# Moving the product with A between the two tiles of every pair, and reordering the prologue of an AdaLN + LoRA feed-forward kernel

## What is computed

```
cond  = grouped_conv1d(x, weight, taps=9, pad=4, groups=4) + (cond_128 @ c_weight.T)[:, :, None] + fside_S_0[None, :, None]
base  = cond @ kernel + bias                        # kernel is 1024 x 1024
A_eff = einsum('bn,nri->bri', gate, lora_A)         # 8 batches of 8 samples, rank 32
B_eff = einsum('bn,nor->bor', gate, lora_B)
delta = (cond @ A_eff.T) @ B_eff.T + (cond @ lora_A_shared.T) @ lora_B_shared.T
out   = x + base + delta
```

## Time and profile before

| | us |
|---|---|
| median of 3 runs (lowest, highest) | 515.07 (512.89, 516.81) |
| the profiled execution | 516.11 |
| its span, first to last instruction | 514.3 |

### The profile page before, as it was taken

The page is one execution under the profiler, slowest core; times in us unless marked ns, Lnnn a source line. Parts: engine busy times, 40 slices in busy tenths (PEclk is TensorE's granted clock), DMA queues, the critical chain, the costliest instruction groups (busy, mean ns, idle before and its releaser), DMA issues.

```text
span 514.3 us, 6831 instructions
## 1 busy us (share of the span) xinstructions
PE 494.3 (96%) x2400; PEld 406.6 (79%) x2400; DVE 342.0 (67%) x389; ACT 165.8 (32%) x207; POOL 269.7 (52%) x154
## 2 busy tenths in 40 slices
PE   4988899989999999999999999999999999999995
PEld 3755598868888888888888888888888888888884
DVE  3988767887938495767948495758848495754411
ACT  2545422341423233331423234331523234331000
POOL 1567861993746338471756347571757247571100
PEclk9999899998999999999999999999999999999999
DMA  8995196852763419331753328331753413232212
GB/s 211 312 234 213 40 264 155 177 203 85 157 164 89 112 43 197 112 105 64 171 155 82 112 54 193 111 100 61 174 152 82 112 50 88 65 97 71 80 40 72
DMA packets 19575, 65.05 MB, mean 126 GB/s; under 512 B 3274, under 2 KB 3914, under 8 KB 18922
## 3 DMA queue, kind: packets, MB, share of 16 engines
q1 hardware_dynamic: 17690, 63.46, 47.1%
q10 hardware_dynamic: 1872, 1.41, 1.1%
HBM read 45.59 MB, written 18.87 MB: 125 GB/s over the span
## 4 chain that ended last, share of the span: by engine, by line
PE 89%; DVE 6%; POOL 1%; DMA 1%; issue 1%; ACT 1%; ACTq 0%; DVEq 0%
PE main L926 65%; PE rank L939 6%; PE main L931 3%; PE conv L856 3%; PE conv L880 2%; PE conv L881 2%; PE conv L882 2%; PE spare L882 1%; PE spare L881 1%; PE spare L880 1%; DMA cw_nat<-in_L_cond_c_weight 1%; DVE y_lo L666 1%; POOL y_lo L379 1%; DVE w_raw L678 1%; POOL x_lo L367 1%
## 5 line engine op out<-in xcount | busy, mean ns | idle before, releaser
L926 PE MATMUL main<-w_hi,y_hi 128*128 128x512 f32 x512 | 160.8, 393 | 1.8 <-POOL w_lo L384 1.1
L926 PE MATMUL main<-w_lo,y_hi 128*128 128x512 f32 x512 | 159.8, 391 | 0.4 <-POOL w_lo L384 0.4
L926 PE MATMUL main<-w_hi,y_lo 128*128 128x512 f32 x512 | 159.5, 390 | 0.0
L379 POOL TENSOR_TENSOR y_lo<-y_stage,y_hi 128x512 fp32r<-128x512 f32 x56 | 89.0, 1611 | 85.5 <-ACT y_hi L481 85.5
L926 PEld LDWEIGHTS main<-w_lo,y_hi 128*128 128x128 f32 x512 | 96.6, 189 | 21.7 <-POOL w_lo L384 0.8
L926 PEld LDWEIGHTS main<-w_hi,y_hi 128*128 128x128 f32 x512 | 95.9, 189 | 22.5 <-issue 2.5
L926 PEld LDWEIGHTS main<-w_hi,y_lo 128*128 128x128 f32 x512 | 96.4, 188 | 20.5
L367 POOL TENSOR_TENSOR x_lo<-x_tr,x_hi 128x1024 fp32r<-128x1024 f32 x28 | 82.2, 2935 | 21.4 <-ACT x_hi L494 21.4
L365 POOL TENSOR_TENSOR xd_lo<-xd,xd_hi 128x512 fp32r<-128x512 f32 x28 | 45.7, 1634 | 55.0 <-ACT xd_hi L492 55.0
L494 ACT ACTIVATE x_hi<-x_tr 128x1024 fp32r<-128x1024 f32 x28 | 57.4, 2049 | 30.2 <-DVE x_tr L642 30.2
L481 ACT ACTIVATE y_hi<-y_stage 128x512 fp32r<-128x512 f32 x56 | 35.5, 633 | 95.6 <-DVE y_stage L660 95.6
(11 more groups left out here) (104 smaller groups left out, 496.0 us busy)
## 6 DMA issues: line engine op xcount, KB each, us to landing
res<-in_x SPq DMA_DIRECT2D x32, 512.0 KB
out<-res SPq DMA_DIRECT2D x31, 512.0 KB
x_in<-in_x SPq DMA_DIRECT2D x28, 512.0 KB, 11.8
w_raw<-in_L_ffn_kernel SPq DMA_DIRECT2D x16, 256.0 KB, 18.6
b_cur<-b_scratch SPq DMA_DIRECT2D x21, 128.0 KB, 2.4
la<-in_L_ffn_lora_A SPq DMA_DIRECT2D x4, 512.0 KB, 10.4
lb<-in_L_ffn_lora_B SPq DMA_DIRECT2D x1, 2048.0 KB, 18.0
b_scratch<-be_hi SPq DMA_DIRECT2D x4, 256.0 KB, 8.6
```

The source lines that it names most:

```text
L379: nc.gpsimd.tensor_tensor(y_parity(y_lo, h, t, e), y_staged(e), y_parity(y_hi, h, t, e).bitcast(F32), ALU.subtract).then_inc(ylo_done, 1)
L926: mm(main[t][:, n * 512:(n + 1) * 512], lhs, rhs[:, k, n * 512:(n + 1) * 512], start=k == 0 and first, stop=False)
```

## The change

1. In every unit PE's `with_a(h)` moves from behind k = 3 of tile 0 to behind k = 7, between the tiles; `fast` of tile 0 stays where it was. `lowrank(0)` moves behind k = 2 of tile 1, `fast` of tile 1 follows it. ACT, DVE and POOL lists follow: the y parts of tile 0 come first, then the rank steps, then x; in unit 1 ACT does both `x_high(2, 0, t)` ahead of `ax_high(1)`, DVE both `x_diff` ahead of `ax_steps(1)`.
2. `chunk(k)` of the prologue does the two products with the rounded W (`w_hi`) for both tiles first and waits for `w_lo` only then; `chunk(1)` and `chunk(2)` are ahead of `convolve(0, 0, 2)` and `(0, 0, 3)`.
3. DVE does `w_add(0..3)` and the `a_turn`s ahead of `x_turn(0, 4..7)`.
4. The low parts of y of unit 0 (`y_first_low`, four subtractions of 128x512) move from DVE to POOL (`y_low_first`); POOL's order of `be_low(0)` and w_low(4..6) shifts. The low part of t01 stays on DVE but moves to behind `finish(0, 1)`; ACT keeps a copy of the raw taps for it (`t01_kept`, one more 128x512 pass).

The diff, cut to its core:

```
@@ POOL
+            def y_low_first(i):
+                t, mh = FIRST[i]
+                pool.wait_ge(yhi_done, i + 1)
+                nc.gpsimd.tensor_tensor(y_part(y_lo, 0, t, mh), y_stage[:, i % 2, :],
+                                        y_part(y_hi, 0, t, mh).bitcast(F32), ALU.subtract).then_inc(y0_lo, 1)
...
             pool.wait_ge(bias_split, 2)
+            y_low_first(0)
+            y_low_first(1)
             w_low(0)
             w_low(1)
             x_first_low(1)
             w_low(2)
+            y_low_first(2)
             w_low(3)
+            y_low_first(3)
+            w_low(4)
             x_low_second(0)
-            w_low(4)
+            w_low(5)
             x_low_second(1)
             a_low(0)
-            w_low(5)
-            w_low(6)
-            for b4 in range(RQ):
...
+            be_low(0)
+            w_low(6)
+            for b4 in range(1, RQ):
+                be_low(b4)
             w_low(7)
@@ ACT
             nc.scalar.activation(t01_hi[:, :, :, :], t01_raw[:, :, :, :], ACT.Copy).then_inc(t01_split, 1)
+            nc.scalar.activation(t01_kept[:, :, :, :], t01_raw[:, :, :, :], ACT.Copy).then_inc(t01_split, 1)
...
             def unit(b, h, y=True, low=True, rank_first=True):
                 u = b * 2 + h
-                if rank_first:
-                    ax_high(u)
-                if low and h == 1:
-                    a_high(b + 1)
-                if y:
-                    for t in range(2):
+                for t in range(2):
+                    if y:
                         y_high(u + 1, 1 - h, 2 * t)
                         y_high(u + 1, 1 - h, 2 * t + 1)
-                        if low:
-                            x_high(u + 2, h, t)
+                    if t == 0 and rank_first:
+                        ax_high(u)
+                        if low and h == 1:
+                            a_high(b + 1)
+                    if low:
+                        x_high(u + 2, h, t)
...
-            ax_high(1)
             x_high(2, 0, 0)
             x_high(2, 0, 1)
+            ax_high(1)
+            a_high(1)
@@ DVE
             y_tile(0, 0, 1, FIRST, first=True)
+            a_turn(0)
             nc.vector.tensor_tensor(t01_raw ...
-            dve.wait_ge(x_first[1], 64)
-            x_turn(0, 4)
-            a_turn(0)
-            x_turn(0, 5)
             a_turn(1)
-            y_first_low(0)
-            y_first_low(1)
-            x_turn(0, 6)
-            x_turn(0, 7)
             w_add(0)
             w_add(1)
             a_turn(2)
-            a_turn(3)
             w_add(2)
             w_add(3)
-            x_first_low(1)
+            a_turn(3)
+            dve.wait_ge(x_first[1], 64)
+            for c in range(XH, XC):
+                x_turn(0, c)
             w_add(4)
             w_add(5)
+            x_first_low(1)
...
             def unit(b, h, y=True, turn=True, begun=False):
+                if begun:
+                    finish(b, 2 * h)
+                if y:
+                    y_pair(nb, nh, 0)
                 if not begun:
                     ax_steps(u)
-                if y:
-                    y_pair(nb, nh, 0)
                 if turn and h == 0:
                     x_turns(b + 1, 0, XC)
-                finish(b, 2 * h)
+                if not begun:
+                    finish(b, 2 * h)
...
             finish(0, 1)
+            dve.wait_ge(t01_split, 2)
+            nc.vector.tensor_tensor(t01_lo[:, :, :, :], t01_kept[:, :, :, :], t01_hi[:, :, :, :].bitcast(F32), ...
             x_turns(1, 0, XC)
             x_diff(2, 1, 0, 0)
+            x_diff(2, 1, 0, 1)
             ax_steps(1)
-            x_diff(2, 1, 0, 1)
@@ PE
             mix_a(2)
-            mix_a(3)
             merge(2)
             merge(3)
+            mix_a(3)
...
+            def chunk(k):
+                pe.wait_ge(y0_lo, 2 if k < 4 else 4)
+                pe.wait_ge(whi_done, k + 1)
+                for t in range(2):
+                    if k == 0 and t == 1:
+                        pe.wait_ge(a_done, RQ)
+                    dense(0, t, k, products=(0, 2))
+                pe.wait_ge(wlo_done, k + 1)
+                for t in range(2):
+                    dense(0, t, k, products=(1,))
...
+            chunk(0)
             merge(4)
             merge(5)
+            chunk(1)
             convolve(0, 0, 2, FIRST, first=True)
-            chunk(1)
             merge(6)
             merge(7)
+            chunk(2)
             convolve(0, 0, 3, FIRST, first=True)
-            chunk(2)
...
                 for k in range(4):
                     dense(h, 0, k)
+                if y and not late:
+                    fast(nb, nh, 0)
+                for k in range(4, KC):
+                    dense(h, 0, k)
                 pe.wait_ge(ylo_done, u * CT)
                 pe.wait_ge(acur_done, b + 1)
                 pe.wait_ge(ax_summed, u)
                 with_a(h)
-                if y and not late:
-                    fast(nb, nh, 0)
-                for k in range(4, KC):
-                    dense(h, 0, k)
-                pe.wait_ge(axlo_done, u + 1)
-                ...
-                lowrank(0)
                 pe.wait_ge(main_free, u * 2)
...
                 for k in range(3):
                     dense(h, 1, k)
+                first_rank()
                 if y:
                     fast(nb, nh, 0 if late else 1)
-                for k in range(3, 5):
+                for k in range(3, 6):
                     dense(h, 1, k)
                 if y and late:
                     fast(nb, nh, 1)
-                for k in range(5, KC):
+                for k in range(6, KC):
                     dense(h, 1, k)
                 lowrank(1)
```

More of the change, by code:

```diff
@@ L97, in adaln_ffn @@
         a_cur = sb("a_cur", [P, KC, 2, R], F32R)
-        t01_hi, t01_lo = sb("t01_hi", [P, G, J, CG], F32R), sb("t01_lo", [P, G, J, CG], F32R)
+        t01_hi = sb("t01_hi", [P, G, J, CG], F32R)
+        t01_kept, = early(("t01_kept", [P, G, J, CG], F32))
+        t01_lo = sb("t01_lo", [P, G, J, CG], F32R)
         lb, = early(("lb", [P, 2, 2048], F32))
@@ L400, in _, with be_low @@
             w_low(2)
+            y_low_first(2)
             w_low(3)
+            y_low_first(3)
+            w_low(4)
             x_low_second(0)
-            w_low(4)
+            w_low(5)
             x_low_second(1)
             a_low(0)
-            w_low(5)
-            w_low(6)
-            for b4 in range(RQ):
+            def be_low(b4):
                 pool.wait_ge(be_hid, b4 + 1)
@@ L417, in unit @@
                 u = b * 2 + h
-                if low and h == 1:
-                    a_low(b + 1)
-                if y:
-                    for t in range(2):
+                for t in range(2):
+                    if y:
                         y_low(u + 1, 1 - h, 2 * t)
                         y_low(u + 1, 1 - h, 2 * t + 1)
-                        if low:
-                            x_low(u + 2, h, t)
+                    if low and h == 1 and t == 0:
+                        a_low(b + 1)
+                    if low:
+                        x_low(u + 2, h, t)
             x_low(2, 0, 0)
@@ L661, in y_pair @@
                                         y_add[:, e, :].rearrange("p (a m n) -> p a n m", a=2, n=SB)).then_inc(y_turned, 1)
[L663 to L667, removed]
             def x_first_low(half):
@@ L793, in _ @@
             finish(0, 1)
+            dve.wait_ge(t01_split, 2)
+            nc.vector.tensor_tensor(t01_lo[:, :, :, :], t01_kept[:, :, :, :], t01_hi[:, :, :, :].bitcast(F32),
+                                    ALU.subtract).then_inc(t01_split, 1)
             x_turns(1, 0, XC)
             x_diff(2, 1, 0, 0)
+            x_diff(2, 1, 0, 1)
             ax_steps(1)
-            x_diff(2, 1, 0, 1)
             unit(0, 1, begun=True)
@@ L874, in fast @@
                     pe.wait_ge(conv_free, 2 * CT)
-                    pe.wait_ge(t01_split, 2)
+                    pe.wait_ge(t01_split, 3)
                 for part in (SUM, EVEN, ODD):
@@ L954, in _ @@
             mix_a(2)
-            mix_a(3)
             merge(2)
             merge(3)
[L959 to L964, removed]
-            pe.wait_ge(t01_sum, 1)
[L968 to L975, removed]
+            mix_a(3)
[7 more added lines that the diff above has]
+                pe.wait_ge(wlo_done, k + 1)
+                for t in range(2):
+                    dense(0, t, k, products=(1,))
+            pe.wait_ge(t01_sum, 1)
+            chunk(0)
             merge(4)
             merge(5)
+            chunk(1)
             convolve(0, 0, 2, FIRST, first=True)
-            chunk(1)
             merge(6)
             merge(7)
+            chunk(2)
             convolve(0, 0, 3, FIRST, first=True)
-            chunk(2)
             merge(8)
@@ L1007, in _ @@
             convolve(0, 1, 3)
-            chunk(7, (0,))
+            pe.wait_ge(wlo_done, KC)
+            dense(0, 0, KC - 1)
```

(19 more changed lines are left out.)

8 lines of the change are left out of this document (1 added, 7 removed).

## The result

Five runs of each kernel on one chip: 512.79 us median (512.05 to 513.78) against 516.81 (512.89 to 517.16), a ratio of 0.9938, 95% interval 0.9911 to 0.9966 (the two medians alone give 0.9922). The kernel is faster by 0.6%, 3.2 us by that ratio, where 7.4 had been forecast.

A forecast was written before the change was run, and what follows sets the result against it. PE works in 96% of the span, so only its waits, slow clock and two ends can be won back. Unit 2 -3.7, unit 1's earlier start -5.4, a clock fall +1.7: -7.4, from 515.07 to 507.7 us, range 503.5 to 512.

The forecast's parts named there:

- Unit 2's wait and clock, -3.7: In unit 2, `with_a`'s wait for POOL's `y_lo` and the slow clock behind it go: -3.7 us.
- The short run ahead of `lowrank(0)` costs nothing in the steady state: Steady units: 4.10 us of matmuls cover a rank chain of 2.16 us, slack 1.9, so price nothing, 14 times.
- Unit 1 begins at 72.4: End of prologue: POOL's list frees main[0] at 72.4, so unit 1 begins then and not at 77.85: -5.4 us.
- PE's own list ends at 70.2: End of prologue: PE's work from B_eff's turns at 53.6 takes 16.5 us, so PE then waits 2.2 us.
- The clock after that wait, +1.7: Start of unit 1: PE's wait of 2.2 us lowers the clock, charged +1.7 us (bounds 0 and 1.7).
- R3: Unit 1: rank chain misses its 0.4 us slack before `lowrank(0)`; 2.4 wait plus 1.7 clock, 511.8 us; chance 0.10.
- R2: Prologue: `lb`, issued later, lands at 50.0 instead of 45.25; PE arrives at 74.9, two clock falls, 510.2 us; chance 0.10.
- DVE is relieved by the move of y's low parts: Prologue: DVE loses four subtractions to POOL, one of which took 3.38 us beside POOL's `x_lo`; POOL gains 5.2 us.

The follow-up runs named there:

- experiment 7: Only the units' new lists on the prologue of before, with the old order in unit 1, against the kernel before: 511.62 us, ratio 0.9922.
- experiment 8: Changed kernel with `lowrank(0)` behind one chunk of tile 1 instead of three, in every unit but the last: 531.52 us, ratio 1.0304 to the kernel before.
- experiment 5: Changed kernel with the old order in unit 1 and POOL waiting for DVE's rank low part ahead of `y_low_second(0)`: 508.16 us, ratio 0.9861 to the kernel before.
- experiment 3: The new prologue alone, with the units' order of before, against the kernel before: 513.52 us, ratio 0.9945.
- experiment 2: All new unit lists, with the new order in unit 1, on the prologue of before, against the kernel before: 517.21 us, ratio 1.0021.
- experiment 4: Changed kernel with POOL waiting for DVE's low part of unit 0's rank product ahead of `y_low_second(0)`: 512.24 us, ratio 0.9936 to the kernel before.
- Experiment 1: Changed kernel with unit 1's old order, rank steps ahead of the second x step on ACT and DVE: 510.22 us, ratio 0.9889 to the kernel before.
- experiment 6: As experiment 5, but the four low parts of y of unit 0 back on DVE: 507.77 us, ratio 0.9845 to the kernel before.
- 9: As experiment 5, with DVE's `finish(0, 0)` ahead of `y_tile(0, 1, 3)`: 506.95 us, ratio 0.9827 to the kernel before.
- experiment 10: As experiment 5, with `mix_b` behind chunk 4 instead of chunk 3: 507.37 us, ratio 0.9838 to the kernel before.

## Why the prediction was wrong

507.7 us with a range of 503.5 to 512.0 was forecast and 512.79 measured: the direction was right, the size more than twice too large (7.4 against 3.2 us by the ratio).

- **Unit 2's wait and clock, -3.7:** right. Shown by the trace after and alone by experiment 7 (4.0).
- **The short run ahead of `lowrank(0)` costs nothing in the steady state:** right. Units are 28.75 apart, and the slack that was put at 1.9 us measured 1.8 (experiment 8).
- **"Unit 1 begins at 72.4":** wrong by 2.3 us in the profiled execution, and this is the first step that failed. POOL's list was right: `y_low_second(0)`, the first of the two `y_lo` from 66.73, ended near 68.0, as worked out. But DVE's list had a second claim that was left out, put at nothing without a reason: its rank subtraction L766 stands between `y_tile(0, 1, 1)` and `y_tile(0, 1, 2)`, and beside a POOL that never pauses it took 4.06 us, so the eviction that was to be done by 68 began at 69.64. The sum had priced such a meeting in unit 1 and in the steady units, and not here, where POOL was said in the same paragraph to have no gap. Where the meeting ended at the first boundary, by chance (experiment 8: 1.31 us, unit 1 at 72.28) or by the wait put on POOL (experiment 5: 2.30 us, unit 1 at 73.22), unit 1 began earlier.
- **"PE's own list ends at 70.2":** wrong by 2.1 us. It ended at 72.27 (71.63 + 0.64): the wait for `lb` took 1.6, and the convolution behind B_eff's turns began at 55.24 where 53.6 was worked out. So PE could not have begun unit 1 before 72.3 in any case; that experiment 8 meets the 72.4 to 0.1 us is in part luck, since it has hardly any of the 2.2 us of wait that went with it.
- **The clock after that wait, +1.7:** charged, and in this execution it did not fall (in experiment 3 it did, at the same place). It came behind the second wait instead. The forecast had read one such wait in the trace of before; that trace has another, of 1.6 us at 52, with a clock of 0.50 behind it.
- **R3, given 0.10, is what happened,** and this is the second and larger failure: a term of 4.65 us that the sum had at nothing. Its price of 4.1 us (2.4 + 1.7) measured 4.65 (2.96 + 1.7). The step that failed is the 0.4 us of slack on which it was set aside, and the meeting that decided it lies one step ahead of the one that R3 names. DVE's second x step asked 0.2 us after POOL had begun an `x_lo` and lost 2.6 us, and L766 met the next `x_lo` and lost 1.2 more (1.58 against 0.42); the rank chain ended 20.0 us after the unit's start where 16.4 had been worked out. The wait is in all four traces with this order (3.0 here, 2.9, 3.5 and, with less cover, 5.7 in experiments 2, 4 and 8). A slack smaller than the error of the times that make it is no slack; the chance should have been far above 0.10. Experiment 1 shows the cause, experiment 2 that the prologue has no part in it.
- **R2, `lb`:** the bound near 45 held roughly. Issued 5 us later, it landed at 46.6 instead of 45.3, and PE waited 1.6 us, not 0.9. So the landing followed the 5 us of issue by 1.3 only; that the wait would be hidden behind POOL held just barely, as PE's list above shows.
- **DVE is relieved by the move of y's low parts (rows 5):** the cost was read rightly and put down to the wrong thing. It came from the meeting with `x_lo`, and in the new order DVE pays none even with the four subtractions on its list (experiment 6). The rule of the Trainium skill (SBUF — State Buffer, Who interferes with whom), that such an instruction waits until POOL's has finished, agrees with 3.74 beside 2.97 and with 3.38 beside 2.98; by it L766 would, as an estimate, wait for the rest of one `w_lo`, 1.3 us, and take 1.7 in all. It did just that in experiment 8 (1.0 us of `w_lo` left, 1.31 in all); the 4.06 measured here says that it can also be passed over at the end of one.

## What to carry to other kernels

When a product is moved to take a wait away, follow every list up to the first unit as well: the steady state was forecast to 0.03 us, and the error lay in the start of unit 1 (2.4 us) and in unit 1 itself (4.65), where two steps had been turned round by hand, less the 1.7 charged for a clock that did not fall there. Mark each instruction of DVE with two SBUF inputs that falls beside a POOL with no gap, and give it, as the upper bound, the length of POOL's whole run. A wait on POOL ends such a meeting at the first boundary (all six traces that have it), but its gain alone was too small for these runs to show (0.9936 with it, 0.9938 without). Undo each reordering by itself: here 0.6% was gained as written, 1.1% with one order put right, 1.4% with one wait on POOL besides, and 1.7% with one more step of DVE moved; the intervals of the last three overlap.

## What the runs showed that had not been expected

**A DVE instruction can be passed over more than once, and need not be.** L766 (32x256, two SBUF inputs) asked while `w_low(7)` ran. With POOL's list as in the change it was passed over at the end of that `w_lo` and between the two `y_lo` behind it in three of four traces, and served only when POOL had nothing ready: 4.06 us after, 3.22 in experiment 1, 4.46 in experiment 3, with POOL at its usual speed (2.61, 2.54 and 2.54 for two). In the fourth, experiment 8, it was let in at the first boundary (1.31), and there the two `y_lo` took 2.73. In all four, and in all six traces with the wait on POOL, it ended 0.27 to 0.29 us after the POOL instruction that it stood beside last. The 128x512 subtractions of DVE were let in at the first boundary (3.38 beside 2.98), and there POOL's next one was stretched (a `w_lo` of 2.81 instead of 2.38). Size alone is not the difference, since the same L766 went both ways; what decides it was not tried and stays open.

**The clock behind a wait is a matter of chance in a middle range.** Of PE's waits in these profiles, apart from the first of each (7.3 to 7.8 us, before which PE had done nothing), none up to 1.4 us brought the granted clock down; of those from 1.6 to 2.4 us six did (1.6 and 2.0 before, 1.6 in experiment 2, 2.4 in 3, 1.9 in 4, 1.8 in 9) and seven did not (1.6 and 2.4 after, 2.4 and 1.7 in 1, 2.0 in 3, 1.6 in 7, 1.8 in 8); of those of 2.9 us and more all four did (after, 2, 4, 8). A fall costs 1.6 to 1.8 us (1.6 in experiment 4; 3.74 less the wait of 1.98 before). The wait for `w_raw`, 1.6 us each time, brought one before and in experiment 2 and none in experiment 7. This is why the kernel before spreads over 512.9 to 517.3 us on one chip, its mean clock being 0.999 in its fastest runs and 0.990 to 0.993 in its slowest, and it is the likely reason that experiment 10, where the wait for `lb` is gone, has all its runs within 0.7 us: a wait of this middle range is worth its length and, on average, about half a fall.
